# Pairwise field interactions: one unit of 32x64 tiles for the inner pairs of two neighbouring chunks

## The reference

```python
e = jnp.stack([tbl_f[ids[:, f]] for f in range(40)], axis=1)          # 2048 x 40 x 32
xi, xj = e[:, iidx, :], e[:, jidx, :]                                 # the 780 pairs i < j
z = jnp.einsum('bpd,pde,bpe->bp', xi, bilinear_matrices, xj)          # 2048 x 780
h = jnp.concatenate([z, dense_ctx], axis=1)                           # 2048 x 796
h = jnp.maximum(h @ W_top1 + b_top1, 0.0)                             # 512
h = jnp.maximum(h @ W_top2 + b_top2, 0.0)                             # 256
y = h @ W_top3                                                        # 1
```

## Time and profile before

| | |
|---|---|
| median of three runs | 1263.33 us |
| the profiled execution | 1266.12 us, span 1264.3 us |
| TensorE busy, weight loads busy | 902.1 us (71%), 328.6 us |
| VectorE, ScalarE, GpSimd busy | 564.9, 81.2, 503.5 us |
| granted TensorE clock | 0.796 in the mean |
| first work behind the first look-up | 163 us |
| blocks 0 to 4, from dense features to dense features | to about 450, 714, 949, 1148 and 1245 us |

### The profile page before, as it was taken

How to read it: one execution, slowest core, us unless ns; L and a number is a source line. 1 busy time by engine, 2 the same in 40 slices (tenths; PEclk the granted TensorE clock), 3 DMA queues, 4 the chain that set the end, 5 groups by cost and what they waited for, 6 DMA issues and landing times.

```text
span 1264.3 us, 18015 instructions
## 1 busy us (share of the span) xinstructions
PE 902.1 (71%) x7934; PEld 328.6 (26%) x7934; DVE 564.9 (45%) x623; ACT 81.2 (6%) x143; POOL 503.5 (40%) x535
## 2 busy tenths in 40 slices
PE   3111135668655867779867858669999899999999
PEld 1000012224332312223212312112222222224445
DVE  2000023225433523447645514437775467786662
ACT  2000020000000000000000000000000000001101
POOL 7777455652444265534324366443224420000000
PEclk7555556667777967769877967779999889999999
DMA  3003001120122200000100010000000000000000
GB/s 64 13 13 52 9 10 20 28 36 18 29 39 52 72 12 11 10 8 8 13 7 9 6 13 11 8 8 7 5 5 9 10 5 2 1 1 3 2 2 2
DMA packets 60880, 20.04 MB, mean 16 GB/s; under 512 B 46359, under 2 KB 59996, under 8 KB 60802
## 3 DMA queue, kind: packets, MB, share of 16 engines
q0 software_dynamic: 16896, 8.68, 5.0%
q1 hardware_dynamic: 43892, 10.18, 4.2%
q10 hardware_dynamic: 14, 0.03, 0.0%
HBM read 18.81 MB, written 0.04 MB: 15 GB/s over the span
## 4 chain that ended last, share of the span: by engine, by line
PE 61%; another core or an unknown queue 20%; issue 12%; DVE 3%; ACT 2%; DMA 1%; SPq 0%; ACTq 0%; DVEq 0%
PE U L653 24%; PE bank_z L670 17%; PE misc L700 10%; PE misc L609 6%; PE U L632 4%; DVE prod L562 3%; PE U L700 1%; DVE ones L541 0%; SPq L304 0%; DMA W<-_L_rec_bilinear_matrices 0%; PE bank_z L678 0%; ACT x_T L431 0%; ACT W L473 0%; DMA idx<-in_ids 0%
## 5 line engine op out<-in xcount | busy, mean ns | idle before, releaser
L389 POOL DMA_INDIRECT rows<-in_tbl,idx x528 | 502.7, 952 | 540.9 <-PE U L632 388.5
L562 DVE TENSOR_TENSOR prod<-U,x_T 128x1024 f32<-128x1024 f32 (+1 forms) x380 | 403.7, 1100 | 329.3 <-remote 174.8
L653 PE MATMUL U<-x_T,W 32*128 32x512 f32 (+1 forms) x1696 | 289.1, 600 | 107.8 <-issue 73.8
L670 PE MATMUL bank_z<-prod,select 128*32 128x512 f32 (+1 forms) x2100 | 267.9, 567 | 3.6 <-issue 3.5
L609 PE MATMUL misc<-ones,tabs 125*32 125x512 bf16 (+1 forms) x1050 | 124.7, 404 | 156.4 <-issue 153.9
L653 PEld LDWEIGHTS U<-x_T,W 32*128 32x128 f32 x1696 | 107.1, 203 | 257.8 <-issue 167.2
L562 DVE TENSOR_TENSOR prod<-U,x_look 128x1024 f32<-128x1024 f32 (+1 forms) x110 | 103.6, 968 | 137.0 <-PE U L653 80.1
L541 DVE TENSOR_SCALAR ones<-idx_wide,row_of 125x2048 bf16<-125x2048 f16 (+3 forms) x100 | 58.4, 604 | 208.1 <-remote 167.5
L700 PE MATMUL misc<-z,W 128*32 128x512 f32 (+1 forms) x952 | 138.3, 566 | 6.1 <-issue 4.3
L609 PEld LDWEIGHTS misc<-ones,tabs 125*32 125x32 bf16 x1050 | 47.4, 109 | 233.2 <-issue 216.4
L670 PEld LDWEIGHTS bank_z<-prod,select 128*32 128x32 f32 x2100 | 51.9, 114 | 186.1 <-issue 131.8
(11 more groups left out here) (48 smaller groups left out, 83.3 us busy)
## 6 DMA issues: line engine op xcount, KB each, us to landing
rows<-in_tbl,idx POOLq DMA_INDIRECT x528
idx_wide<-idx_rows SPq DMA_DIRECT2D x3, 500.0 KB
idx_wide<-idx_rows SPq DMA_DIRECT2D x3, 375.0 KB
W<-in_W_top SPq DMA_DIRECT2D x1, 512.0 KB
idx_wide<-idx_rows SPq DMA_DIRECT2D x2, 187.5 KB
W<-in_W_top SPq DMA_DIRECT2D x11, 32.0 KB
prod<-in_tbl SPq DMA_DIRECT2D x2, 156.2 KB
z<-in_tbl SPq DMA_DIRECT2D x2, 156.2 KB
```

Source lines behind the costliest of these rows:

```text
L389: nc.gpsimd.indirect_dma_start(out=rows[:, n % R_SLOTS, t, f, :], out_offset=None, in_=tables[field][:, :], in_offset=bass.IndirectOffsetO ...
L562: last = nc.vector.tensor_tensor(prod[:, (2 * g + h) % P_SLOTS, 0:R, m * N:(m + n) * N].rearrange("p r (m n) -> p r m n", m=n), U[:, at:at ...
L653: last = nc.tensor.matmul(U[:, at + r % 2, m * N:(m + 1) * N], W[r * DIM:(r + 1) * DIM, at_W:at_W + P], x_of(o, a)[r * DIM:(r + 1) * DIM, ...
L670: last = nc.tensor.matmul(bank_z[r * DIM:(r + 1) * DIM, 0:N], sel, prod[:, (2 * g + r // 2) % P_SLOTS, r % 2, m * N:(m + 1) * N], start=(k ...
```

## The change

The inner pairs of two neighbouring chunks a and a+1 (a even) share the unit (a, a). Its 4 x 2 tiles of 32x64 hold 12 matrices: the six pairs of chunk a, and in the other places the six of chunk a+1 with its fields in reverse order. Units (a, a) with odd a are gone: 50 units a block, and 25 cycles in blocks 0 and 4, 50 in the others. For a = 0 the shared unit stands first among its units, for the other even a last. Such a unit has 8 matmuls in `project` and 4 in `sum_up`. Its moving and multiplying operands are partly in `x_twin`, which ScalarE fills by 7 copies a unit (25 units), three iterations ahead where the turn allows it. VectorE multiplies it by three instructions in place of two in each of two diagonal units. SyncE loads all `W` before the later wide index rows, in 66 loads in place of 39, and the first network layer by 97 - 4 = 93 loads in place of 67. The look-up of group 1 for block 2 moves from block 0 to block 1.

The core of the diff ("..." marks what is left out):

```diff
+def units_of(a):
+    twin = [(a, a)] if a % 2 == 0 else []
+    across = [(a, J) for J in range(CHUNKS - 1, a, -1)]
+    return across + twin if a else twin + across
...
-place([("look", o, q) for o, q in ((1, 0), (0, 1), (2, 0), (1, 1), (3, 0), (2, 1))], 0, FIRST_CYCLE[1])
-place(mlp_jobs(0, (0, 1)) + [("look", 4, 0)] + mlp_jobs(0, (2, 3)) + [("look", 3, 1)] + mlp_jobs(0, (4, 5, 6))
-      + [("look", 4, 1)], FIRST_CYCLE[1], FIRST_CYCLE[2] - 1)
+place([("look", o, q) for o, q in ((1, 0), (0, 1), (2, 0), (1, 1), (3, 0))], 0, FIRST_CYCLE[1])
+place(mlp_jobs(0, (0, 1)) + [("look", 2, 1)] + mlp_jobs(0, (2, 3)) + [("look", 4, 0)] + mlp_jobs(0, (4, 5))
+      + [("look", 3, 1)] + mlp_jobs(0, (6,)) + [("look", 4, 1)], FIRST_CYCLE[1], FIRST_CYCLE[2] - 1)
...
+TWINS = [(o, a) for o in range(BLOCKS) for a in CHUNK_OF_STEP if a % 2 == 0]
+TWIN_CYCLE = [CYCLE_OF[(o, UNITS.index((a, a)))] for o, a in TWINS]
...
+    TWIN_AT[max(_turned, TWIN_CYCLE[_n] - 3)].append(_n)
...
+            def copy_twin(n):
+                (o, a), N = TWINS[n], ROWS[TWINS[n][0]]
...
+                if n:
+                    act.wait_ge(multiplied, 2 * (TWIN_CYCLE[n - 1] + 1))
...
+                for r in range(CF):
+                    nc.scalar.activation(x_twin[r * DIM:(r + 1) * DIM, 1, 0:N],
+                                         x_of(o, a + 1)[(CF - 1 - r) * DIM:(CF - r) * DIM, :], ACT.Copy)
+                for r in range(2):
+                    nc.scalar.activation(x_twin[r * DIM:(r + 1) * DIM, 0, 0:N],
+                                         x_of(o, a + 1)[(CF - 1 - r) * DIM:(CF - r) * DIM, :], ACT.Copy)
+                nc.scalar.activation(x_twin[2 * DIM:, 0, 0:N], x_of(o, a)[2 * DIM:, :], ACT.Copy
+                                     ).then_inc(twin_copied, 1)
...
             load_dense(0)
             load_wide(2, 0)
-            load_W(5)
+            for c in range(5, CHUNKS):
+                load_W(c)
             load_wide(1, 1)
-            load_W(6)
             load_wide(3, 0)
-            load_W(7)
-            load_wide(2, 1)
-            load_W(8)
-            load_wide(4, 0)
-            load_W(9)
...
+                    if UNITS[ks[m]][0] == Js[m]:
+                        if h == 0:
+                            nc.vector.tensor_tensor(to[:, 0, m * N:(m + 1) * N], U[:, at, m * N:(m + 1) * N],
+                                                    x_of(o, Js[m]), ALU.mult)
+                            last = nc.vector.tensor_tensor(to[:, 1, m * N:(m + 1) * N],
+                                                           U[:, at + 1, m * N:(m + 1) * N],
+                                                           x_twin[:, 0, 0:N], ALU.mult)
+                        else:
+                            last = nc.vector.tensor_tensor(to[:, :, m * N:(m + 1) * N],
+                                                           U[:, at:at + 2, m * N:(m + 1) * N],
+                                                           x_twin[:, :, 0:N], ALU.mult)
...
+                for k in ks:
+                    if UNITS[k] == (a, a):
+                        pe.wait_ge(twin_copied, TWINS.index((o, a)) + 1)
...
+                            for side in range(2):
+                                own = side == 0 and r == 0 or side == 1 and r < CF - 1
+                                x = x_of(o, a)[row, :] if own else x_twin[row, 1, 0:N]
+                                last = nc.tensor.matmul(U[side * P // 2:(side + 1) * P // 2, at + r % 2,
+                                                          m * N:(m + 1) * N],
+                                                        W[row, at_W + side * P // 2:at_W + (side + 1) * P // 2], x,
+                                                        start=True, stop=True, skip_group_check=True)
...
-                    for r in rows_of(k):
+                    for r in range(CF):
```

More of the change, by code:

```diff
@@ L30 @@
 CHUNK_OF_STEP = [CHUNKS - 1 - c for c in range(CHUNKS)]
-UNITS = [(a, J) for a in CHUNK_OF_STEP for J in range(CHUNKS - 1, a - 1, -1)]
+def units_of(a):
+    twin = [(a, a)] if a % 2 == 0 else []
+    across = [(a, J) for J in range(CHUNKS - 1, a, -1)]
+    return across + twin if a else twin + across
+UNITS = [u for a in CHUNK_OF_STEP for u in units_of(a)]
 NU = len(UNITS)
-FIRST_UNIT = [UNITS.index((a, CHUNKS - 1)) for a in CHUNK_OF_STEP]
+FIRST_UNIT = {c: UNITS.index(units_of(a)[0]) for c, a in enumerate(CHUNK_OF_STEP) if units_of(a)}
 UPT = 8
@@ L37 @@
 DENSE_SLOT = UPT - 1
-assert NU % UPT == UPT - 1 and DENSE == CF * CF
+assert NU % UPT < UPT and NU % UPT and DENSE == CF * CF
 def slot_runs():
@@ L46, in slot_runs @@
             js = [UNITS[k][1] for k in ks if UNITS[k][0] == a]
+            first = min([k for k in ks if UNITS[k][0] == a], default=0) - t * UPT
+            if a in js:
+                runs.append((t, a, a, a, first))
+                js.remove(a)
+                first += 1
             if js:
-                first = min(k for k in ks if UNITS[k][0] == a) - t * UPT
                 runs.append((t, a, min(js), max(js), first))
@@ L54 @@
 SLOT = {(a, J): slot + J - lo for _, a, lo, hi, slot in RUNS for J in range(lo, hi + 1)}
-def rows_of(k):
-    a, J = UNITS[k]
-    return range(CF - 1) if a == J else range(CF)
-def half_rows(ks, h):
-    return [r for r in range(2 * h, 2 * h + 2) if any(r in rows_of(k) for k in ks)]
+assert len(SLOT) == NU
 CYCLES, FIRST_CYCLE = [], []
@@ L84, in pair, with w_col, back_pairs @@
     return i * (FIELDS - 1) - i * (i - 1) // 2 + (j - i - 1)
-W_WIDTH = [P * (CHUNKS - a) for a in CHUNK_OF_STEP]
+W_WIDTH = [P * len(units_of(a)) for a in CHUNK_OF_STEP]
 W_START = [sum(W_WIDTH[:c]) for c in range(CHUNKS)]
 W_COLS = sum(W_WIDTH)
+def w_col(a, J):
+    return W_START[CHUNK_OF_STEP.index(a)] + P * (J - a - (a % 2))
+def back_pairs(a):
+    return [(CF - 1 - f, CF - 1 - g, pair(CF * (a + 1) + f, CF * (a + 1) + g))
+            for f in range(CF) for g in range(f + 1, CF)]
+W_LOADS = [0 if a == CHUNKS - 1 else CF + (len(back_pairs(a)) if a % 2 == 0 else 0) for a in CHUNK_OF_STEP]
 W1_LOADS = []
@@ L97 @@
             W1_LOADS.append((_t, DIM * (_i - CF * _a) + CF * _slot + _j - CF * _lo, pair(_i, _j), CF * _hi + CF - _j))
+    if _lo == _a:
+        for _r, _q, _p in back_pairs(_a):
+            W1_LOADS.append((_t, DIM * _r + CF * _slot + _q, _p, 1))
 for _r in range(CF):
@@ L159 @@
 TABS_SPLIT_AT = 1
-TURN_AT = {g: [] for g in range(-1, G)}
+TURN_AT = {g: [] for g in range(-2, G)}
 for _o in range(BLOCKS):
@@ L475, in _ @@
                                  ).then_inc(W1_zeroed, 1)
-            for g in range(-1, G + 1):
+            for g in range(-2, G + 1):
                 if g == TABS_SPLIT_AT + 1:
@@ L484, in _ @@
                     break
-                for kind, o, j, i in MISC_AT[g]:
+                for kind, o, j, i in MISC_AT.get(g, []):
                     if i == JOB_PARTS[(kind, o, j)] - 1:
@@ L492, in _ @@
                     keep_turn(o, c)
+                for n in TWIN_AT[g]:
+                    copy_twin(n)
             for j in range(RESULTS):
@@ L512, in _ @@
             to_half(0, ROWS[0] // P).then_inc(idx_h_made, 1)
-            for c in range(CHUNKS):
-                zero = nc.vector.memset(W[:, W_START[c]:W_START[c] + P], 0.0)
+            for a in range(0, CHUNKS, 2):
+                zero = nc.vector.memset(W[:, w_col(a, a):w_col(a, a) + P], 0.0)
             zero.then_inc(W_zeroed, 1)
@@ L724, in _ @@
             pe.wait_ge(constants, 1)
-            for g in range(-1, G):
-                if g + 1 < G:
+            pe.wait_ge(idx_T_made, 1)
+            for g in range(-2, G):
+                if 0 <= g + 1 < G:
                     project(g + 1)
```

85 lines of the change are left out of this document (54 added, 31 removed).

## The result

The changed kernel takes 1255.87 us (median of 20 runs), the kernel before 1265.24, timed beside it: ratio 0.9918, interval 0.9898 to 0.9939. That is faster, by 9.4 us where 20 were forecast; the interval is 8 to 13 us. The profiled execution took 1248.72 us, one of the lower ones, so its distance of 17 us to the one before is nearly twice the gain.

What follows compares the result with a forecast made beforehand. TensorE's free work between turns was taken as the savable bound, with TensorE crawling while GpSimd gathers. 44 - 14 - 10 + 3 - 3 = 20 us off the profiled 1266.1 gives 1246, forecast 1243 us by median; range 1222 to 1266.

Steps and rivals of the forecast that it cites:

- extra 0: Shared unit's `project` in 512-column blocks: all eight tiles run side by side, 1.07 us as now, so no added time.
- The sides take turns: Rival, every shared `project`: the two 64-column sides alternate, costing 21 us plus about 5, giving 1269 us; chance 0.17.
- the rival of a free change: Rival: changing tile width between 128 and 64 columns costs nothing; 46 us saved in all, near 1220 us; chance 0.18.
- the price of a unit: Removed diagonal units on TensorE: 2.07 us each, 10.4 us per 512-block, 31.0 us for three blocks.
- the sign that I gave: Blocks 1 to 3 each get shorter by 6 to 9 us, blocks 0 and 4 by little.
- The clear part: Block 3 after the last gather: five fewer cycles of unchanged 2.07 and 2.93 us; no shortening would prove the forecast wrong.
- Total 10 us: TensorE's waits on ScalarE's 175 copies, mainly for chunk 0 in each block: 10 us, between 0 and 15.
- The wait at chunk 0: TensorE waits for kept turn and copies: 2.3 us in each 512-block, 0.6 us in each 256-block.
- The start is no worse: Kernel start: first turn comes one `project` earlier; the 2.7 us of copies fill time TensorE spends idle afterwards.
- Lost by merging 3: Fewer cycles between turns push gathers together where GpSimd then bounds: 3 us lost, between 0 and 15.
- a term that I had at 3: TensorE's 11.1 us wait for chunk 0's `W` goes, but crawling would follow: 3 us gained, between 0 and 11.
- The gathers hide it: Rival: GpSimd ends each stretch until 1050 us, so only later savings count, some 5 us, 1259 us; chance 0.17.

Runs made afterwards that it cites:

- e10: Changed kernel with no change of tile width inside a cycle and chunk 0's turn two iterations earlier: 1252.94 us, ratio 0.9781 to the kernel before.
- e1: Kernel before without its 528 gathers, the row buffers filled once with a constant: 768.86 us.
- e3: Changed kernel without gathers and without ScalarE's 175 copies into `x_twin`, which is filled once with a constant: 708.39 us.
- e2: Changed kernel without its 528 gathers, the row buffers filled once with a constant: 733.15 us.
- e4: Changed kernel with its gathers but without ScalarE's 175 copies into `x_twin`: 1229.63 us, ratio 0.9797 to the kernel before.
- e9: Changed kernel itself, unchanged, timed again on the third chip: 1276.65 us against 1282.14 for the kernel before, ratio 0.9909.
- both edits together: Changed kernel with no tile-width change inside a cycle plus chunk 0's turn two iterations earlier: 1252.94 us, ratio 0.9781; on another chip 763.05 us, 0.981.

## Why the prediction was right in sign and wrong in size

**Sign, bound and the priced units: right.** The shared `project` is 1.05 us at 512 columns (forecast 1.07, extra 0), the sides run together, and *The sides take turns* is refuted. At 256 columns it is 2.44 (forecast 2.5), and e10 shows that it is the change of width; the rival of a free change falls. The Trainium skill, "TensorEngine Tiling (Array Packing)", Key Properties, says that a change of mode drains TensorE, and the runs agree between 32x128 and 32x64: four pieces of 0.6 us, 2.44 in all, against 1.08 without a change.

**The units.** Without gathers, and without the copies (e1 to e3), blocks 1 to 3 get 4.9, 12.7 and 11.7 us shorter, 29.3 in all where 31 were forecast, though block 1 has taken over a look-up from block 0. So the price of a unit was right where TensorE runs freely. With the gathers the sign that I gave, 6 to 9 us in each of these blocks, came in one of three: from dense features to dense features the profiles have 4.7, 9.7 and 4.1 us, of a pair that is 17 us apart.

**The clear part.** Forecast: five fewer cycles in block 3's clear part. I had said I would be wrong if it didn't get shorter, and it didn't. From the last gather to the end of block 3, before and after:

```profile
1045.00:1148.50 103.50, 103.45 (x881) 30.92 (x877) 80.35 (x74) 8.28 (x14) 0.03 (x1) 1.00 0.01 1
```

```profile
1028.70:1133.20 104.50, 100.70 (x920) 30.57 (x920) 80.07 (x75) 21.31 (x38) 0.00 (x0) 1.00 0.01 2
```

The stretch holds 39 records more, so TensorE has less of its work behind it when the last gather ends. The turn that releases it is placed by cycles, and there are fewer of them. The clear part is no fixed piece of the program. Block 4 went from 96.9 to 94.8 us between its last matmuls, 2.1 shorter, where 1 longer was forecast. All that follows the last gather gained 219.2 - 218.4 = 0.8 us; everything else was gained ahead of it.

**The step that failed: "Total 10 us" for ScalarE.** It measured 24.8 us where TensorE runs freely (e2 to e3), and with the gathers 15, between 9 and 22 (e4). So it is the term that failed, and the best value puts half of the missing 10 us there. The wait at chunk 0 was right in a 512-block (2.3 forecast, 2.49 measured), but block 0's was 3.77 and not 0.6, and the first shared unit of a block, which I charged once (block 2, 2 us), waits in three. "Most copies start three iterations before the unit, 6 to 9 us, and are hidden" was the sentence behind that. "The start is no worse" was wrong as well: without gathers TensorE waits 8.0 us for the first copies. With them the first `project` starts at 167.31 us, at 164.39 without the copies (e4) and at 163.75 before.

**"Lost by merging 3": perhaps the other half.** All that isn't the copies was forecast at 44 - 14 + 3 - 3 = 30 us; e4 measures 0.0203 x 1259 = 25.6, and its interval is 20 to 31. So the best values leave 4 us more lost than I took, inside of my bound of 15, but 0 isn't excluded. That the whole gain is about half of the forecast is shown; how the missing half divides between the copies and this term is not.

Without gathers and copies the change saves 60.5 us (e1 to e3), 30 more than forecast. Most of that is block 0, 29 us shorter where I had priced about zero. Only a part of it is the units: e1 waits 10.0 us there for `W`, a term that I had at 3, and the look-up of group 1 for block 2 has left the block. Under the gathers block 0 ends at 438 us after and 434 before. Part of the reason is that the gathers have moved: turns are placed by cycles, and 332 us of block 0 are bursts where 311 were, while blocks 2 and 3 have 123 and 38 where they had 132 and 47.

Two mechanisms for the cover stand in the traces, not separated by a run. The first I named and then left out of the sum, that where TensorE crawls by the record nothing changes. The shared unit has as many records as two diagonal ones, so a cycle saved in the crawl would save nothing. A burst's length follows from its gathers (16 take 20 us, 8 take 10). Of the kernel before, by the start of each record, 801 of 1797 fall into a burst in block 0, 750 of 1712, 619 of 1428 and 296 of 1436 in blocks 1 to 3: 45, 44, 43 and 21%. Of the 10.4 us in each of blocks 1 to 3 that is (0.44 + 0.43 + 0.21) x 10.4 = 11.2. But most of these records pass in the first 6 us of a burst, at no crawl. Counting only what starts later, 18, 18 and 7%, gives 4.5. Both are estimates from counts. The second mechanism is new: `z` is kept after eight units, of 50 and no longer of 55, at other places against the bursts, and under a burst ScalarE's copy comes late. TensorE's matmuls wait 9.9 us for it in the profile after, 21.8 in e9, none before. But they wait 25.4 us for it in e10, which beats the change, so this wait doesn't rank the versions by itself. My sentence on `z` looked only for copies ahead of it in ScalarE's queue.

**W.** The wait went, as forecast. Its 3 us weren't tested on the long kind.

**The gathers hide it** had 0.17 and 1259 us. On the short kind it holds in the main. On the long kind the time lies nearer to its 1259 than to 1243, but its mechanism fails: of its two signs the first was met (GpSimd's waits shrank from 388.5 to 370 in profiles that are 17 us apart), and the second was not, since the last gather ended at 1028.6 in place of 1045.0. So the gain lies ahead of the last gather, where the rival has none. That 1255.87 us lies inside of my range shows little: it ran from 1222 to 1266 and held several mechanisms. And my rival of a free change of width should have stood at 1217 and outside of it, since its 46 us were taken off the profiled execution and not off the median.

What stays open: how the missing 10 us divide between the copies and the gathers, and the cover between the two mechanisms; why the change saves so little at half of the gathers; and what sets whether a chip crawls. That both edits together save 16 us on the long kind needs no further cause: waits of 8.8 (3.77 + 2.50 + 2.49) and block 4's 5.4, seen in the traces, make 14.2.

## What to carry to other kernels

Before you price a removed piece, ask in which stretches it runs: where a stretch's length is set by another engine and yours goes by the instruction, count records and not microseconds, and look whether that holds for the whole stretch or, as here, only behind its first 6 of 20 us; and ask which other engine's short step, held back in the same stretch, the new order will wait for. Copies that stand between a transpose and their first use cost what of their length the distance doesn't cover (4.8 us against one iteration: 2.49 us of wait), each time, even on an engine that is 14% busy; moving the producer earlier removed these waits (e10), though alone it was worth only 0 to 3 us on the short kind. And in this kernel tiles of one width inside of a cycle are worth more than the plain unit's wider tile.

## What the runs showed of the hardware

The crawl belongs to the chip and not to the program alone: two chips showed it and two didn't. With the same 528 gathers at the same pace (7.6 of 10 us busy) TensorE does 152 matmul records in 10 us on one chip and, at its lowest, 9 on another, and the kernel before takes 778 or 1282 us. The second of these rows, e9 on the third chip:

```profile
250.00:260.00 10.00, 4.59 (x9) 1.18 (x8) 0.48 (x1) 0.00 (x0) 7.56 (x9) 0.51 0.93 108
```

The DMA engines are busy there (0.93) with more than the gathers; the kernel before does 18 records at a DMA share of 0.08, so the crawl needs no such load.

The clock doesn't explain it. The stretch from 20 to 120 us, in e9 at half of the full clock (1.2 GHz) and in e10 at all of it (2.4 GHz):

```profile
20.00:120.00 100.00, 16.29 (x56) 4.79 (x56) 3.28 (x10) 0.00 (x0) 75.75 (x80) 0.50 0.17 26
```

```profile
20.00:120.00 100.00, 16.09 (x46) 4.30 (x47) 2.11 (x4) 0.00 (x0) 75.58 (x80) 1.00 0.09 13
```

56 and 46 records in 100 us. No row names what TensorE waits for. Nor does the crawl end with the issuing: in the kernel before the last of the first 114 gathers is issued by 146.8 us, and TensorE's next `project` starts at 163.75. So whether the issuing slows TensorE or the transfers behind it stays open. A ranking of two versions can therefore differ between chips: W's loads alone equal the whole change on one kind.

Tiles that are split in rows and columns at once overlap: 16 records of 32x64 tiles with 512 columns in 1.05 us, as long as 8 of 32x128.
